# Gated cross-attention and quantised FFN block on one core: a quarter-wise hand-over of q and k, transposed scores taken by quarter, and a new slot order on every engine

## What is computed

```python
x = x + jnp.tanh(g_xattn[0]) * _L0_xattn_ref(_layernorm(x), ctx_512, Wq, Wkv_expand, Wout)
x = x + jnp.tanh(g_ffn[0]) * _L0_ffn_ref(_layernorm(x), w_gate_up, w_down)

# _L0_xattn_ref: 16 heads of 32 channels, causal
qp = q @ Wq.T;  k, v = jnp.split(latent_kv @ Wkv_expand.T, 2, axis=-1)
scores = jnp.einsum('bhqd,bhkd->bhqk', qh, kh) / sqrt(32)      # masked where k > q
out = jnp.einsum('bhqk,bhkd->bhqd', softmax(scores), vh)
return out @ Wout.T

# _L0_ffn_ref: rows of x, w_gate_up, h and w_down are rounded to 127 steps of their maximum
h = silu(gate) * up;  return quant(h) @ quant(w_down).T
```

## Time and profile before

| | us |
|---|---|
| median of 3 runs (813.43, 814.57, 826.63) | 814.57 |
| the profiled execution's own time | 820.32 |
| its span, first to last instruction | 818.3 |
| mean granted TensorE clock (share of 2.4 GHz) | 0.946 |
| PE, DVE, ACT, POOL busy | 737.9, 621.2, 413.8, 575.7 |

### The profile page before, as it was taken

How to read it: one execution, slowest core, us unless ns; L and a number is a source line. 1 busy time by engine, 2 the same in 40 slices (tenths; PEclk the granted TensorE clock), 3 DMA queues, 4 the chain that set the end, 5 groups by cost and what they waited for, 6 DMA issues and landing times.

```text
span 818.3 us, 16788 instructions
## 1 busy us (share of the span) xinstructions
PE 737.9 (90%) x5345; PEld 525.0 (64%) x5345; DVE 621.2 (76%) x1894; ACT 413.8 (51%) x657; POOL 575.7 (70%) x766
## 2 busy tenths in 40 slices
PE   3488889999999999999999998788599999999994
PEld 3477768878878878878887876554244444444441
DVE  4554758977977878887887784536689999999982
ACT  5335656576576566567567444233344433444440
POOL 5435666787787777777787755453478888888885
PEclk9688999999999999999999996789799999999997
DMA  6787758868868868868866767931246656666655
GB/s 222 182 177 182 164 139 210 196 187 210 197 180 224 184 187 217 195 179 211 221 167 182 186 146 157 234 99 65 63 95 153 147 144 138 148 150 150 145 129 164
DMA packets 137870, 137.57 MB, mean 168 GB/s; under 512 B 90269, under 2 KB 99767, under 8 KB 137655
## 3 DMA queue, kind: packets, MB, share of 16 engines
q1 hardware_dynamic: 136720, 135.97, 66.8%
q10 hardware_dynamic: 1063, 0.54, 0.3%
HBM read 40.24 MB, written 25.31 MB: 80 GB/s over the span
## 4 chain that ended last, share of the span: by engine, by line
PE 80%; issue 6%; POOL 4%; DMA 4%; DVE 4%; ACT 2%; SPq 0%; ACTq 0%; POOLq 0%; DVEq 0%
PE psum L1149 18%; PE psum L1006 10%; PE psum L1071 10%; PE psum L1028 10%; PE psum L1164 8%; PE psum L1045 5%; PE psum L959 5%; PE psum L957 4%; PE psum L1016 3%; PE psum L993 3%; PE psum L1047 2%; DMA qs<-nmT 2%; PE psum L944 1%; DMA x1b<-x_scratch 1%; PE psum L980 1%
## 5 line engine op out<-in xcount | busy, mean ns | idle before, releaser
L760 DVE CUSTOM_DVE_ANT_0 junk<-psum,mask 128x128 f32<-128x128 f32 (+1 forms) x512 | 153.7, 353 | 91.6 <-PE psum L959 89.6
L1149 PE MATMUL psum<-w1q,xqb 128*128 128x512 bf16 (+1 forms) x768 | 161.2, 367 | 14.0 <-DVE gate L899 11.5
L504 POOL TENSOR_TENSOR up<-gate,up 128x512 f32<-128x512 f32 (+1 forms) x96 | 112.4, 1185 | 53.8 <-ACT gate L700 42.7
L1149 PEld LDWEIGHTS psum<-w1q,xqb 128*128 128x128 bf16 x768 | 75.4, 99 | 98.0 <-issue 19.1
L607 ACT ACTIVATE prob<-psum 128x768 f32<-128x768 f32 x128 | 103.5, 809 | 54.1 <-PE psum L1047 54.0
L705 ACT ACTIVATE up<-up,round_bias,hinv 128x1408 f32<-128x1408 f32 x32 | 50.0, 1561 | 127.9 <-DVE hinv L923 127.9
L430 POOL TENSOR_SCALAR_AFFINE_SELECT prob<-prob 128x512 f32<-128x512 f32 x128 | 81.3, 639 | 44.2 <-ACT prob L607 42.9
L438 POOL TENSOR_TENSOR prob<-prob 128x256 f32<-128x256 f32 x128 | 94.2, 741 | 6.8
L1164 PE MATMUL psum<-w2q,hqT 128*128 128x512 bf16 x352 | 83.4, 388 | 6.1 <-DMA hqT<-hq 6.1
L1006 PE MATMUL psum<-xT_hi,wq_hi 128*128 128x256 f32 x256 | 76.5, 299 | 10.0 <-POOL xT_lo L445 10.0
L957 PE MATMUL psum<-ks,qs 96*128 96x128 f32 x256 | 70.6, 276 | 16.0 <-issue 13.2
(11 more groups left out here) (116 smaller groups left out, 1811.0 us busy)
## 6 DMA issues: line engine op xcount, KB each, us to landing
qs<-q_hi SPq DMA_DIRECT2D x128, 128.0 KB, 2.4
ks<-k_hi SPq DMA_DIRECT2D x128, 128.0 KB, 4.4
xln<-x_dram SPq DMA_DIRECT2D x16, 512.0 KB, 4.7
qs<-q_lo SPq DMA_DIRECT2D x64, 128.0 KB, 3.2
ks<-k_lo SPq DMA_DIRECT2D x64, 128.0 KB, 4.0
x<-x_dram SPq DMA_DIRECT2D x16, 512.0 KB, 3.7
x_scratch<-x SPq DMA_DIRECT2D x16, 512.0 KB, 4.4
x1b<-x_scratch SPq DMA_DIRECT2D x32, 256.0 KB, 3.4
```

The costliest lines, as they stand in the source:

```text
L504: pool.tensor_tensor(up[:, t % 3, o], gate[:, t % 3, o], up[:, t % 3, o], ALU.mult).then_inc(f["prod_done"], 1)
L760: dve.tensor_tensor_reduce(junk[:, n % 2, 0:w], psum[:, h % 2, cols], m, 1.0, LOWEST, ALU.add, ALU.max, mx[:, X % 2, t, h:h + 1]).then_inc ...
L1149: last = pe.matmul(psum[:, n, 0:w], xqb[:, t % 4, k, :], w1q[:, k, half * I + o:half * I + o + w], start=(k == 0), stop=(k == KH - 1))
```

## The change

No matmul, copy or DMA of q, k or v is added or removed. What changes is which heads stand together, when the transfers may go and what they are waited for, and the order of steps.

1. **By quarter.** `score_pair(X, pair)` takes places 2·pair and 2·pair + 1 of `qs` and `ks`, which belong to one quarter (two g with the same j). `weigh(X, j)` then has the four heads of quarter j. The channels of the attention output are therefore ordered by j first, and the rows of Wout are loaded in that order, by four DMAs in the place of one.
2. **Freed and awaited by quarter.** `spread_heads` becomes `spread_quarter`, which waits for the two pairs of the batch two before that use this quarter, and issues 1 or 2 DMAs. There are 16 semaphores (q or k, parity, quarter). `scores` waits at heads 0, 4, 8 and 12 for that quarter's moves alone; `high_q`, `split_q`, `high_k` and `low_k` wait for all four quarters of the batch before.
3. **New order** of all steps in `slot` on SP, PE, DVE, ACT and POOL, and another table `WORK`. Queries of batch b + 2 all come in slot b (before, the first two groups of batch b + 3 ended slot b). The plain scores start after the second pair; `maxima_rows` comes before the outputs. The pieces of FFN weights go through one slot later.

```diff
-    MOVES = 3 * BLOCKS
+    MOVES = 3
...
-        WORK = [("V", 0, 1, 7), ("V", 1, 1, 6), ("Q", 1, 2, 7), ("K", 0, 2, 6), ("K", 1, 2, 7), ("T", 0, 3, 6),
-                ("O", 0, -1, 6), ("T", 1, 3, 7), ("O", 1, -1, 7), ("Q", 0, 3, 6)]
+        WORK = [("Q", 0, 2, 6), ("Q", 1, 2, 7), ("V", 0, 1, 7), ("V", 1, 1, 6), ("K", 0, 2, 7), ("K", 1, 2, 6),
+                ("O", 0, -1, 6), ("T", 0, 3, 7), ("T", 1, 3, 6), ("O", 1, -1, 7)]
...
-                def spread_heads(src, ready, dst, pieces, moved, batch):
+                def spread_quarter(src, ready, dst, pieces, sems, batch, j):
                     if present(batch):
-                        sp.wait_ge(ready, 2 * batch + 2)
-                        wait_for(sp, s["st_done"], PAIRS * (batch - 1))
+                        if j == 0:
+                            sp.wait_ge(ready, 2 * batch + 2)
+                        if batch >= 2:
+                            sp.wait_ge(s["st_done"], PAIRS * (batch - 2) + 2 * j + 2)
                         for piece in pieces:
-                            for j in range(BLOCKS):
-                                sp.dma_start(dst[HD * piece:HD * (piece + 1), batch % 2, GROUPS * j:GROUPS * (j + 1), :].bitcast(F32),
-                                             src[HD * j:HD * (j + 1), :, :].bitcast(F32)).then_inc(moved, DMA)
+                            sp.dma_start(dst[HD * piece:HD * (piece + 1), batch % 2, GROUPS * j:GROUPS * (j + 1), :].bitcast(F32),
+                                         src[HD * j:HD * (j + 1), :, :].bitcast(F32)).then_inc(sems[batch % 2][j], DMA)
...
                 def scores(X, h):
                         if h == 0:
-                            pe.wait_ge(s["q_moved"], DMA * MOVES * (X + 1))
-                            pe.wait_ge(s["k_moved"], DMA * MOVES * (X + 1))
                             wait_for(pe, s["mt_copied"], X)
                             wait_for(pe, s["on_done"], 2 * (X - 1))
+                        if h % GROUPS == 0:
+                            pe.wait_ge(q_moved[X % 2][h // GROUPS], moved(X))
+                            pe.wait_ge(k_moved[X % 2][h // GROUPS], moved(X))
...
                 def score_pair(X, pair):
-                    g, j = pair // 2, 2 * (pair % 2)
-                        h, bank = GROUPS * (j + d) + g, 2 + d
+                        h, bank = 2 * pair + d, 2 + d
```

More of the change, by code:

```diff
@@ L177, in gated_block @@
         s = {n: sem("a_" + n) for n in names}
+        q_moved = [[sem(f"a_q_moved{p}{j}") for j in range(BLOCKS)] for p in range(2)]
+        k_moved = [[sem(f"a_k_moved{p}{j}") for j in range(BLOCKS)] for p in range(2)]
         f = {n: sem("f_" + n) for n in """w1_loaded w2_loaded steps_loaded x_loaded0 x_loaded1 x_loaded2 x_loaded3
@@ L180, in gated_block, with moved, wait_moved @@
             hinv y_done prod_done hq_done out_done stored0 stored1""".split()}
+        def moved(batch):
+            return DMA * MOVES * (batch // 2 + 1)
+        def wait_moved(eng, sems, batch):
+            if batch >= 0:
+                for j in range(BLOCKS):
+                    eng.wait_ge(sems[batch % 2][j], moved(batch))
         def present(batch):
@@ L839, in slot @@
                 def slot(b):
-                    measure(b - 2, 1)
-                    split_q(b + 2, 0)
+                    residual(b - 2, 1)
                     if b < B:
@@ L844, in slot @@
                         normalise(b - 1, 1)
+                    measure(b - 2, 0)
+                    maxima(b + 1, 0)
                     measure_x(b + 3)
@@ L851, in slot @@
                             dve.memset(ks[3 * HD:3 * HD + 2, par, :, :].bitcast(F32), 1.0).then_inc(s["ones_set"], 1)
-                    if b < B:
-                        low_o(b - 1, 0)
-                    maxima(b + 1, 0)
-                    maxima(b + 1, 1)
+                    for h in range(1, 4):
+                        maxima(b + 1, h)
+                    measure(b - 2, 1)
+                    maxima(b + 1, 4)
+                    split_q(b + 2, 0)
+                    maxima(b + 1, 5)
                     split_q(b + 2, 1)
@@ L861, in slot @@
                         dve.tensor_reduce(lo_rows[:], lo_tab[:], AX.X, ALU.add).then_inc(s["table"], 1)
-                    for h in range(2, 6):
+                    maxima(b + 1, 6)
+                    maxima(b + 1, 7)
+                    if b < B:
+                        low_o(b - 1, 0)
+                    for h in range(8, 12):
                         maxima(b + 1, h)
@@ L880, in slot @@
                     split_reciprocals(b)
-                    residual(b - 1, 1)
-                    measure(b - 1, 0)
                 def last():
```

232 lines of the change are left out of this document (127 added, 105 removed).

## The result

The changed kernel takes 860.0 us in the median (852.33 to 864.33, 4 runs) beside 816.84 us (4 runs) for the kernel before: a ratio of 1.053, 95% interval 1.043 to 1.064. It is slower, and the forecast was 787 with a range up to 808. Some executions of a kernel ran at a lower granted clock and over 1.5% longer than its fastest, and the ratios leave them out, so a ratio need not be the quotient of two medians. The profiled execution took 864.33 us, its span is 862.5.

What follows compares the result with a forecast made beforehand. Steady attention was taken as bound by PE, the filling by one long dependency chain, slots 14 and 15 by waits and clock. Terms -7.5 - 12.8 + 2.0 - 11.5 + 2.5 = -27.3 us on 820.3 gave 793, 787 by the median; range 774 to 808.

Steps and rivals of the forecast that it cites:

- Nothing: Parts costed at no time: four Wout DMAs, extra semaphores, FFN weight pieces one slot later.
- my 29.35: PE's time for one steady slot in the new order: 29.35 us, 30.05 less 0.7 of waiting; no other engine reaches this.
- Rival B: Slower: behind the load of xln in SP's queue, quarters 0 and 1 land late, PE waits; 833; with other losses 0.12.
- Steady slots: Attention's middle slots: the waits ahead of the first plain scores go, -7.5 us.
- Filling: Start up to sp(2), batch 2's transposed scores: earlier plain scores and maxima, shorter slot 1; -12.8 us, bounds -6 and -15.
- Slots 14 and 15: From batch 14's transposed scores to the first FFN matmul: 54 us for 65.5, -11.5 us, decided by SP's chain.
- Passage: Passage to the FFN, tile 0 to tile 2: rounding ahead of statistics, longer half clock; +2.5 us, between 0 and +5.
- Queries moved: Slot 13: 24 query matmuls the old order had already done by sp(2) are still owed; +2.0 us.
- A: Rival: POOL's and SP's slips cancel the steady gain, slow clock in slots 14 and 15 stays; about 802; chance 0.16.
- C: Rival: full clock through slots 14 and 15, shorter SP chain, filling gains 15; 779 and below; chance 0.14.

Runs made afterwards that it cites:

- e1: Changed kernel with SP's store and load of the FFN weight piece moved early, right behind the store of xq; 804.35 us, ratio 0.983 to the kernel before.
- e3: Changed kernel with the weight piece's store and load later on SP, behind two transfers of k_hi's quarter 0; 890.43 us, ratio 1.088 to the kernel before.
- e2: Changed kernel with DVE's residual of the first half batch ahead of the weight piece's row maxima; 823.12 us, ratio 1.000 to the kernel before.
- e6: Kernel before with release and await by quarter alone (plus head pairing and Wout load), old order of steps; 799.1 us, ratio 0.976.
- e7: e1 with the split of the context ahead of the second power on POOL before batch 0; 802.32 us, ratio 0.985 to the kernel before.
- e10: e1 with the transposed load of w2 issued one slot later on SP, behind the residual load; 797.46 us, ratio 0.976 to the kernel before.
- e8: Changed kernel with 16 unread matmuls on PE ahead of the waiting context transposes, batches 0 to 12; 853.03 us, ratio 1.049 to the kernel before.

## Why the prediction was wrong

**The failed step** is the first one under "Nothing": "FFN pieces one slot later (the last one is done a slot before it is needed)". I asked when the last piece is needed and not when, within a slot, each row is. The step that moves a piece issues a store and a load of 512 KB; in the old order the load stood 15.8 us ahead of DVE's use of the row, in the new one 2.2 us ahead of the moment at which DVE was ready for it, with 6.7 to landing. In my new order the step stands behind the load of the residual, at which SP waited 4.4 us for ACT. Costed at nothing, it cost 5.1 us a slot over my 29.35 (some 3.65 of PE's waiting and 1.6 of slower clock), 56 of the 72 us between forecast and measurement, and more than the whole gain. e1 takes back 56 us by moving that one call, and e3 makes it worse by moving it the other way.

**What made it dear** is the queue behind it. On DVE the residual stands behind the row's maxima, and the residual frees the bank for PE's transposes: a late transfer for the FFN, of which nothing is needed for another 200 us, stops attention. e2 shows this: with two steps moved ahead the loss falls by about three quarters. I had checked the new order of each engine for its length (29.35 us for PE, less for the rest), which was right, and not every wait in it for the time between issue and use.

**Rival B** had the right shape and the wrong place. It too blamed SP's in-order queue and a wait each slot, and its 833 came from 3.3 us a slot; I looked for it at the transfers into ks and qs, which are on time (PE has no idle time ahead of the plain scores), and gave it and like losses 0.12.

**Steady slots, -7.5:** right once the load is early. e1 takes 350.1 us from sp(2) to sp(14), against my 352.0 (with the queries moved) and 357.5 before. But the hand-over alone gives it: e6 takes 349.6. My bounds below nothing named only POOL's slips of 0.5 us.

**Filling, -12.8:** -2.1 in the changed kernel, -5.1 in e1. The first plain score came at 43.5, 1.5 us behind my 42; from there to the maxima were 16.6 us and not 14, and from the maxima to sp(0) 6.1 and not 5.5. So sp(0) came at 66.3 and not at 61.5. In e1 slots 0 and 1 then took 27.2 and 31.9 us, for my 26.5 and 29.4. A new wait of 7.95 us ahead of the keys of batch 0 looked like the cause, and e7 shows that by itself it is not. The old order gets as far, 125.9 (e6).

**Slots 14 and 15, -11.5:** -5.3 after, -7.2 in e1, -9.7 in e10. The mis-sized terms are those of SP's chain: the load of w1 was issued 16.2 us after sp(14) (552.05) and not 12, and from there to the end of w2's issue were 24.0 us and not 21.2; together 7 us, where tile 0 came 6.2 us later than forecast. The granted clock was 0.87 from sp(14) to sp(15) and 0.77 from there to tile 0, for 0.73 and 0.75 before. The old order with the hand-over gets -9.0 (e6), so this gain too is not one of the new order. **Passage, +2.5:** +1.5, within its bounds, but I had PE idle for 8 to 10 us ahead of tile 0, and it idled 1.43 there and 5.83 ahead of the broadcasts; the number came out without its reason. **Queries moved, +2.0:** not told apart. Two sums among the rivals don't close: A's terms, 7.5 and 4 us on 787, give 798.5 and not 802, and C's, 4 and 2.2 us, give 781 and not 779. Neither bears on the outcome.

## What to carry to other kernels

When an in-order queue is rearranged, list for every load in it the time from its issue to its use, before and after, including the loads that serve another stage; one that had 11 us to spare may have none. Look also at which waits the load now stands behind: those count with the issues in front of it. For each instruction that waits for such a load, look at what is queued behind it on its engine: the price of a late transfer is set by that, not by what the transfer is for. And try the idea behind a change without the reordering first: here the hand-over by quarter in the old order gave nearly all there was.

## What the runs showed of the hardware

The same 512 KB load of a row took 4.5 to 5.3 us to landing in the steady slots of the kernel before, 5.2 to 7.1 in the changed one and 5.6 to 7.9 in e1. Only its place in SP's queue, and so what was issued around it, differs between the last two; what sets the time was not isolated, but a margin must allow for the spread. Behind an idle time of 4.05 us of PE the granted clock was 0.50 for 6 us (363 to 369), in other slots of the same run it was low for less long, and behind one idle time of 2.79 us it stayed at 1.00; in e8, with PE busy for 363.5 of 368 us, it stayed at 1.00 from 150 to 518 us. Issuing the transposed loads took SP 11.5 to 14.5 us (w1) and 5.5 to 7.6 us (w2) in the kept traces, and what stands behind them in its queue was issued only then.
